# A four-tap convolution moved from VectorE to ScalarE and GpSimd in a state-space and mixture kernel

## The reference, cut to what matters

```
x0  = layernorm(x)                       # then an RMS norm with norm_scale
xs, res = split(rms(x0) @ w_in)          # 512 channels each
xs  = silu(causal_conv(xs, conv_w, 4 taps per channel) + conv_b);  res = silu(res)
delta, B, C = split(xs @ w_xproj);  delta = softplus(delta @ w_dt + b_dt)
state[c, n, t] = exp(delta * A[c, n]) * state[c, n, t-1] + delta * xs * B[n, t]   # 16 states n
y   = sum_n state * C[n];  out = (y + xs * D) * res
x1  = x + layernorm(x0 + out @ w_out)
u   = layernorm(x1)                      # two branches of 8 gated low-rank experts follow,
f   = experts(u, running sum of u)       # each over the running sum along the tokens
result = x1 + layernorm(f @ W_O)
```

## Time and profile before

| what | value |
|---|---|
| median of three runs | 2573.84 us |
| the profiled execution | 2574.76 us, span from first to last instruction 2572.9 us |
| granted TensorE clock, mean | 0.936 |
| busy share of the span | DVE 89%, PE 85%, POOL 68%, ACT 66% |
| first scan to last scan | 95.8 to 2451.8 us, 16 batches |

### The profile page before, as it was taken

The page is one execution under the profiler, slowest core; times in us unless marked ns, Lnnn a source line. Parts: engine busy times, 40 slices in busy tenths (PEclk is TensorE's granted clock), DMA queues, the critical chain, the costliest instruction groups (busy, mean ns, idle before and its releaser), DMA issues.

```text
span 2572.9 us, 35477 instructions
## 1 busy us (share of the span) xinstructions
PE 2179.5 (85%) x9268; PEld 1305.7 (51%) x9268; DVE 2291.9 (89%) x3172; ACT 1704.3 (66%) x3353; POOL 1752.1 (68%) x1227
## 2 busy tenths in 40 slices
PE   5666788888898988888898888989888888888788
PEld 2434455454554645455464545546454555546454
DVE  1599999999999999999899999999999999999941
ACT  3555585958668594876758586685948767595643
POOL 0759586767858676695867768586766958677611
PEclk9776899999999999999899999999999999999999
DMA  5011010101002011110101011020101001011100
GB/s 123 28 46 30 20 58 25 58 26 54 31 20 64 25 56 29 54 30 26 59 25 55 29 54 31 19 64 25 57 28 54 30 26 58 25 50 32 35 1 17
DMA packets 83383, 101.58 MB, mean 39 GB/s; under 512 B 23480, under 2 KB 49872, under 8 KB 83168
## 3 DMA queue, kind: packets, MB, share of 16 engines
q1 hardware_dynamic: 83168, 99.06, 13.1%
HBM read 90.13 MB, written 8.91 MB: 38 GB/s over the span
## 4 chain that ended last, share of the span: by engine, by line
DVE 33%; issue 28%; POOL 15%; PE 15%; ACT 4%; DVEq 1%; POOLq 0%; ACTq 0%
DVE h L1259 15%; POOL bx L714 9%; DVE yT L1275 9%; PE bank L744 8%; PE stateT L913 3%; DVE xs L1163 3%; DVE prod L1234 2%; PE bank L888 2%; POOL x_back L646 1%; POOL scratch L630 1%; POOL scratch L636 1%; DVE xs L1175 1%; ACT decay L1119 1%; DVE rows L1187 1%; ACT cum_sb L1084 1%
## 5 line engine op out<-in xcount | busy, mean ns | idle before, releaser
L714 POOL TENSOR_TENSOR bx<-dx,B_rows 128x1024 f32<-128x1024 f32 x512 | 1206.6, 2363 | 379.3 <-DVE h L1259 374.7
L1259 DVE TENSOR_TENSOR_SCAN h<-decay,bx 128x512 f32<-128x512 f32 x1024 | 1237.7, 1209 | 57.4 <-ACT decay L1119 50.9
L1119 ACT ACTIVATE decay<-delta,decay_rate 128x512 f32<-128x512 f32 x1024 | 706.6, 692 | 487.3 <-DVE h L1259 477.3
L913 PE MATMUL stateT<-ident,h 128*128 128x128 f32 x4096 | 668.8, 295 | 264.9 <-DVE h L1259 179.5
L913 PEld LDWEIGHTS stateT<-ident,h 128*128 128x128 f32 x4096 | 498.8, 149 | 614.5 <-issue 333.2
L1275 DVE SCALAR_TENSOR_TENSOR yT<-stateT,C_tok,yT 128x512 f32<-128x512 f32 x960 | 697.8, 727 | 34.3 <-PE stateT L913 29.7
L744 PE MATMUL bank<-hT,w_in_sb 128*128 128x512 f32 x512 | 247.5, 621 | 34.7 <-DVE xs L1163 33.7
L744 PE MATMUL bank<-k_to_expert,cumT 128*128 128x512 f32 x512 | 266.4, 647 | 4.1 <-DVE prod L1234 4.1
L744 PE MATMUL bank<-q_to_expert,xnT 128*128 128x512 f32 x512 | 248.0, 608 | 1.9 <-ACT C_tok L1007 1.9
L1084 ACT ACTIVATE cum_sb<-bank,gate 128x64 f32<-128x64 f32 x1024 | 222.7, 328 | 35.6 <-PE bank L744 33.3
L888 PE MATMUL bank<-expert_to_out,prodT 128*128 128x256 f32 x1024 | 241.8, 379 | 0.0
(11 more groups left out here) (162 smaller groups left out, 2412.9 us busy)
## 6 DMA issues: line engine op xcount, KB each, us to landing
B_rows<-B_scratch SPq DMA_DIRECT2D x256, 256.0 KB, 3.2
x_front<-in_L_attn_x SPq DMA_DIRECT2D x16, 512.0 KB, 4.6
x_back<-in_L_attn_x SPq DMA_DIRECT2D x16, 512.0 KB, 4.1
out<-x_back SPq DMA_DIRECT2D x16, 512.0 KB, 3.3
w_in_sb<-in_L_attn_w_in SPq DMA_DIRECT2D x1, 1024.0 KB, 5.9
h<-in_L_ffn_V_fwd SPq DMA_DIRECT2D x2, 256.0 KB
h<-in_L_ffn_W_inv_exp SPq DMA_DIRECT2D x2, 256.0 KB
h<-in_L_ffn_W_fwd SPq DMA_DIRECT2D x2, 256.0 KB
```

The costliest lines, as they stand in the source:

```text
L714: pool.tensor_tensor(bx[use % BX_RING][:, :, :], dx[q.parity][:, 2 * half:2 * half + 2, :], row, ALU.mult).then_inc(s_bx.step(f"{n},{half} ...
L913: last = pe.transpose(stateT[j % 2][:, c * P:(c + 1) * P], h[n % 2][:, c, j * P:(j + 1) * P], ident[:, :])
L1119: act.activation(decay[c % 2][:, :], delta[q.parity][:, c, :], ACT.Exp, scale=decay_rate[:, c, n:n + 1]).then_inc(s_exp.step(f"{n},{c}"), 1)
L1259: dve.tensor_tensor_scan(h[n % 2][:, c, :], decay[c % 2][:, :], bx[(2 * n + c // 2) % BX_RING][:, c % 2, :], 0.0, ALU.mult, ALU.add).then_ ...
```

## The change

Four things change.

- **Convolution.** The DVE tasks cvA, cvB and cvC are gone. A new ACT task `tap` makes, for each group of 128 channels, three products from the same PSUM bank (`Copy` with the tap as scale) into a ring of four rows of `scratch`; a new POOL task `cv` adds each of them to `xs`, shifted. Every add waits for its product and for the add before it. From the fifth product on, ACT waits until POOL has added the product four before. The bank is free after the third product. The silu of ACT waits for POOL's last add, and so do the later writers of `scratch`.
- **Front norm.** ACT sums the rows with an accumulator output (`front_sum`) and then squares `sum - 256 x` with another (`front_square`). The unused elementwise results go to `hT`.
- **Output norm.** The copy from PSUM into `o_rows` becomes an `Identity` with an accumulator output, and four squares (`out_square`) follow. POOL's factor instructions take scales for these sums; their number stays.
- **Beats.** The timetable is new for most tasks.

```diff
-    ("F", "cvA", "dve"): (35, 37, 38, 42),
-    ("F", "cvB", "dve"): (37, 37, 39, 42),
-    ("F", "cvC", "dve"): (37, 37, 40, 44),
+    ("F", "sum", "act"): (5,),
+    ("F", "sq", "act"): (10,),
+    ("F", "tap", "act"): (35, 37, 41, 44),
+    ("F", "cv", "pool"): (40, 41, 44, 57),
-    ("F", "xs", "pe"): (34, 35, 37, 40),
+    ("F", "xs", "pe"): (31, 32, 34, 39),
-    ("F", "res", "pe"): (36, 38, 41, 66),
+    ("F", "res", "pe"): (34, 41, 45, 62),
-    ("B", "rb", "pool"): (300,),
+    ("B", "rb", "pool"): (303,),
     ("B", "t", "act"): (301,),
-    ("B", "st1", "dve"): (302,),
+    ("B", "st1", "dve"): (304,),
-    ("L", "out", "pe"): (373, 381, 393, 398, 431, 434, 439, 443),
+    ("L", "out", "pe"): (373, 381, 394, 397, 434, 437, 439, 441),
-    ("L", "st", "dve"): (455,),
-    ("L", "ag", "dve"): (460,),
+    ("L", "sq", "act"): (448,),
...
+            def conv_task(b, c, use):
+                pool.wait_ge(f_act.sem, f_act.done(b, f"cv{c}"))
+                for back in range(1, TAPS):
+                    product = 3 * c + back - 1
+                    pool.wait_ge(f_act.sem, f_act.done(b, f"tp{c}{back}"))
+                    if back > 1:
+                        pool.wait_ge(f_pool.sem, f_pool.done(b, f"cv{c}{back - 1}"))
+                    pool.tensor_tensor(xs[b.parity][:, c, back:], xs[b.parity][:, c, back:], scratch[:, product % 4, 0:T - back],
+                                       ALU.add).then_inc(f_pool.step(f"cv{c}{back}"), 1)
...
+            def front_sum(b, k, use):
+                act.wait_ge(xf_in, b.count(16, 16))
...
+                for j in range(TB):
+                    act.activation(hT[:, j // 2, j % 2 * D:(j % 2 + 1) * D], x_front[:, j, :], ACT.Identity,
+                                   accum_out=sum_f[:, j:j + 1]).then_inc(f_act.step(f"sm{j}"), 1)
+            def front_square(b, k, use):
+                act.wait_ge(f_act.sem, f_act.done(b, "sm3"))
+                for j in range(TB):
+                    act.activation(hT[:, j // 2, j % 2 * D:(j % 2 + 1) * D], x_front[:, j, :], ACT.Square, scale=-1.0 * D, bias=sum_f[:, j:j + 1],
+                                   accum_out=var_f[:, j:j + 1]).then_inc(f_act.step(f"sq{j}"), 1)
...
+            def tap_task(b, c, use):
+                act.wait_ge(f_pe.sem, f_pe.done(b, f"xs{c}"))
+                for back in range(1, TAPS):
+                    product = 3 * c + back - 1
+                    if product >= 4:
+                        before = product - 4
+                        act.wait_ge(f_pool.sem, f_pool.done(b, f"cv{before // 3}{before % 3 + 1}"))
...
+                    act.activation(scratch[:, product % 4, 0:T - back], use.bank[:, 0:T - back], ACT.Copy,
+                                   scale=conv_w_sb[:, c, TAPS - 1 - back:TAPS - back]).then_inc(f_act.step(f"tp{c}{back}"), 1)
...
             def silu_task(b, k, use):
-                act.wait_ge(f_dve.sem, f_dve.done(b, "cvC3"))
+                act.wait_ge(f_pool.sem, f_pool.done(b, "cv33"))
...
-                act.activation(o_rows[:, j, :], use.bank[:, 0:D], ACT.Copy).then_inc(l_act.step(f"out{j}"), 1)
+                act.activation(o_rows[:, j, :], use.bank[:, 0:D], ACT.Identity, accum_out=sum_o[:, j:j + 1]).then_inc(l_act.step(f"out{j}"), 1)
```

More of the change, by code:

```diff
@@ L112 @@
[L112 to L121, removed]
+    ("F", "dt", "act"): (88, 90, 107, 114),
@@ new lines @@
+    ("F", "ex", "act"): (91, 95, 107, 115),
+    ("F", "ln", "act"): (93, 97, 111, 120),
+    ("F", "w", "pool"): (101, 108, 117, 126),
+    ("F", "w2", "pool"): (101, 109, 125, 126),
+    ("F", "d1", "dve"): (96, 105, 120, 123),
+    ("F", "row", "sp"): (95, 128, 132),
+    ("B", "y", "pe"): (263, 264, 264, 264),
+    ("B", "u", "dve"): (264, 264, 264, 269),
+    ("B", "o", "pool"): (273, 275, 277, 278),
+    ("B", "wo", "pe"): (279, 282, 282, 287),
+    ("B", "r", "dve"): (283, 287, 287, 289),
@@ L157 @@
-    ("L", "out", "act"): (382, 401, 440, 445),
-    ("L", "st", "dve"): (455,),
-    ("L", "ag", "dve"): (460,),
-    ("L", "rs", "pool"): (473,),
+    ("B", "logit", "act"): (342,),
+    ("B", "logit_rows", "pe"): (343,),
+    ("B", "lb", "dve"): (342,),
+    ("B", "mx", "dve"): (342,),
+    ("B", "sub", "pool"): (349,),
+    ("B", "ex", "act"): (345,),
+    ("B", "sm", "dve"): (344,),
+    ("B", "sn", "pool"): (354,),
+    ("B", "rc", "dve"): (345,),
+    ("B", "wa", "pool"): (356,),
+    ("B", "gT", "pe"): (367,),
@@ L283, in program @@
         C_tok = [sb(f"C_tok{i}", P, TB, NS) for i in range(2)]
-        st_f, st_b, st_1, st_o = (sb(f"st_{n}", P, TB, 6) for n in "fb1o")
-        mv_f, mv_b, mv_1, mv_o = (sb(f"mv_{n}", P, TB, 2) for n in "fb1o")
+        st_b, st_1 = (sb(f"st_{n}", P, TB, 6) for n in "b1")
+        mv_b, mv_1 = (sb(f"mv_{n}", P, TB, 2) for n in "b1")
+        sum_f, var_f, sum_o, var_o = (sb(n, P, TB) for n in ("sum_f", "var_f", "sum_o", "var_o"))
         ve_f, ms_f, rs_f, r2_f = (sb(n, P, TB) for n in ("ve_f", "ms_f", "rs_f", "r2_f"))
@@ L593, in prologue, with rstd @@
                                allow_small_or_imprecise_dtypes=True))
-            def rstd(steps, batch, mv, ve, rs, nm, names):
-                pool.tensor_scalar(ve[:, :], mv[:, :, 1], EPS, None, ALU.add).then_inc(steps.step(names[0]), 1)
+            def rstd(steps, batch, mean, var, unit, factor, ve, rs, nm, names):
+                pool.tensor_scalar(ve[:, :], var, unit, EPS, ALU.mult, ALU.add).then_inc(steps.step(names[0]), 1)
                 pool.wait_ge(steps.sem, steps.done(batch, names[0]))
@@ L684, in back_rstd @@
                 pool.sem_inc(passed["pool"], 1)
-                rstd(b_pool, b, mv_b, ve_b, rs_b, nm_b, ("ve", "rb", "ng", "nm"))
+                rstd(b_pool, b, mv_b[:, :, 0], mv_b[:, :, 1], 1.0, minus_one, ve_b, rs_b, nm_b, ("ve", "rb", "ng", "nm"))
             def x1_rstd(b, k, use):
@@ L949, in centre, with out_square @@
                     act.activation(dst[:, j, :], src[:, j, :], ACT.Identity, scale=rs[:, j:j + 1], bias=nm[:, j:j + 1]).then_inc(steps.step(f"{name}{j}"), 1)
+            def front_sum(b, k, use):
+                act.wait_ge(xf_in, b.count(16, 16))
+                if b.turn is not None or b.const > 0:
+                    act.wait_ge(B_out, b.count(16, 0))
+                for j in range(TB):
[6 more added lines that the diff above has]
+                                   accum_out=var_f[:, j:j + 1]).then_inc(f_act.step(f"sq{j}"), 1)
+            def out_square(b, k, use):
+                act.wait_ge(l_act.sem, l_act.done(b, "out3"))
+                for j in range(TB):
+                    act.activation(flat(prodT[:, 2 * j:2 * j + 2, :]), o_rows[:, j, :], ACT.Square, scale=-1.0 * D, bias=sum_o[:, j:j + 1],
+                                   accum_out=var_o[:, j:j + 1]).then_inc(l_act.step(f"sq{j}"), 1)
             def h_task(b, k, use):
@@ L1149, in aggregate @@
                     dve.bn_aggr(mv[:, j, :], st[:, j, :]).then_inc(steps.step(f"{name}{j}"), 1)
-            def front_stats(b, k, use):
-                dve.wait_ge(xf_in, b.count(16, 16))
-                stats(f_dve, x_front, st_f, "st")
-            def front_aggregate(b, k, use):
-                aggregate(f_dve, b, st_f, mv_f, "st", "ag")
-            def tap(back, name, before):
-                def task(b, c, use):
-                    x_c = xs[b.parity][:, c, :]
-                    dve.wait_ge(before[0].sem, before[0].done(b, f"{before[1]}{c}"))
-                    dve.scalar_tensor_tensor(out=x_c[:, back:], in0=use.bank[:, 0:T - back], scalar=conv_w_sb[:, c, TAPS - 1 - back:TAPS - back],
-                                             in1=x_c[:, back:], op0=ALU.mult, op1=ALU.add).then_inc(f_dve.step(f"{name}{c}"), 1)
-                return task
             def d1_task(b, c, use):
```

129 lines of the change are left out of this document (61 added, 68 removed), and 6 rows, old and new, of the table TIMETABLE.

## The result

The changed kernel takes 2507.12 us (median of four runs, 2505.18 to 2508.23) against 2573.85 us, a ratio of 0.9737 with a 95% interval of 0.9712 to 0.9762. The forecast was 2479 us: the sign and the range hold, and the gain is 67 us where 96 were forecast. The profiled execution has a span of 2506.4 us against 2572.9; the mean granted TensorE clock is 0.937 against 0.936, and it is 1.00 in beats 24 to 47 of the batches shown, before and after, so the clock doesn't explain the gain.

The account below looks back on a forecast made before the run. DVE was taken to bound the kernel. Fifteen batches each win 11.2 us less 4.5 given back, and the start costs 5: -96 from 2574.76, so 2479 us; range for 8 in 10: 2408 to 2575.

Parts of the forecast that it names:

- What bounds the kernel: Whole kernel: DVE, busy 2291.9 of 2572.9 us, sets the period; in beats 40 to 47 PE is busy throughout.
- Taken from DVE: Per batch: twelve taps 7.9 us, eight bn_stats 2.6, eight bn_aggr 0.7, together 11.2 us less DVE work.
- Given back in beats 24 to 47: Beats 24 to 47: 4.5 us a batch of the DVE saving lost again, range 3.0 to 6.5.
- The account by PE: Beats 24 to 47: PE still needs 30.5 us where DVE needs 25.7, so 3.0 to 4.8 us come back.
- The account by POOL and ACT: From beat 32's scan: beat 46's exponential queues behind cv2, rb and t, so DVE waits 4.9 us.
- Elsewhere: Beats outside 24 to 47: output statistics' 1.7 us on DVE won, squares covered, front sums, Identity and loads cost nothing.
- The start: First batch: its convolution isn't under a scan, POOL's adds end at 52.7, so 5 us are lost once.
- The rule against it: Convolution adds: two-input elementwise work is about twice as slow on GpSimd; 7.9 us of one engine become 23 of two.
- All of it is won: Rival, chance 0.22: PE and POOL catch up in gaps of other slots, nothing given back, 2412 us.
- ACT as the bound in 64 to 95: Rival, chance 0.10: squares, dearer accumulators and dense silu and gelu give back 4.1 us more a batch, 2541 us.
- The tie of ACT to POOL over the ring of four: Rival, chance 0.20: late POOL holds ACT in its taps, so DVE waits for bx and decay; 2605 us, slower.
- The signs named: Beats 32 to 47 some 22 us, DVE idle 4 to 5; mv_b wait gone; new nm_b wait 3 us or more.

Follow-up runs that it names:

- e3: Changed kernel with POOL's twelve convolution adds cut to 8 columns each, ACT's products, waits and order kept: 2498.55 us, ratio 0.9703 to the kernel before.
- e5: Changed kernel with ACT's t (norm of B) at beat 48 instead of 45, behind the exponentials of beats 46 and 48: 2549.74 us.
- e9: Changed kernel with DVE's sixth expert product moved from beat 38 to 40 and PE's xv0 from beat 95 to 97: 2484.50 us.
- e10: As e9, and DVE's third r task also moved from beat 31 to 33: 2485.88 us, ratio 0.9647 to the kernel before.
- e4: Changed kernel with res projections 0 to 2 (beats 34, 41, 45) over one of two channel halves, less work for PE: 2481.39 us.
- e2: Changed kernel with the statistics of both norms back on DVE at old beats 7, 8, 71 and 76, convolution as changed: 2534.84 us.
- e7: Changed kernel with ACT's eight squares a batch cut from 256 to 8 columns, accumulator reads kept: 2505.19 us.
- e8: Changed code with all tasks common to the old timetable back at their old beats, only new tasks at new beats: 2586.11 us.
- e11: Kernel before with only the convolution moved to ACT and POOL, statistics and all other beats as before: 2604.65 us.
- e1: Changed kernel with the convolution back on DVE at its old beats, statistics on ACT and all other beats as changed: 2690.57 us.
- e6: Changed kernel with the first add of each group over 510 columns instead of 511: 2505.52 us (single run).

## Why the prediction was right, and where it was off

**What bounds the kernel.** Held: DVE was the pace, and with it relieved PE became full in beats 24 to 47, named beforehand as the place.

**Taken from DVE.** Forecast 11.2 us a batch, busy time near 2115 us; measured 2126.1, 10.4 a batch. A little less. An instruction of DVE that waits doesn't overlap the one before it in the records, and such gaps (over 0.06 us) rose from 146 to 273; at the 0.08 us of an overlap that makes 0.6 of the 0.8, an estimate.

**Given back in beats 24 to 47.** Forecast 4.5 us by two accounts. The account by PE was the right one: e3 shows that POOL can be 8.5 us shorter there without effect, e5 that the exponential behind t can be freed without effect, e9 and e10 that PE's list fills the stretch to 28.96 us. It was mis-sized: I took PE's list for 30.5 us from its busy time of before, and it is 29.0. Measured is 3.4. e4 bounds the account: with PE relieved further the stretch shrinks by 0.8 us only. The account by POOL and ACT (4.9 us at the exponential of beat 46) was wrong in size, 0.58 measured. Counted from the scan of beat 32, rb ended at 15.0 us where I had 17.8: three tasks of adds took 3.6 us each and not 4.05, and by starting in slot 24 to 31, where DVE already waited for PE, POOL had won another 1.5. And DVE itself came to this scan at 17.4 and not at 15.6, since it had waited for PE on the way. The twelve adds take 13.8 us a batch, below even the lower end of 14.8 that I gave. That t must stand where it stands, as e5 shows, was not in my account.

**Elsewhere.** This is the largest step that failed in the sum: "Elsewhere ... nothing". DVE's idle time a batch (means of ten batches, gaps over 0.06 us) rose from 7.0 to 11.9 us; 3.4 of it lies in beats 24 to 47, where there was 0.1, so 1.6 came up in other slots: +0.8 in 64 to 71 (exponential behind ACT's dense tasks: I had counted the output norm's statistics on DVE as won, and e2 shows that those in this slot were covered by ACT's silu), +1.25 in 96 to 103 (transposes behind xv0, which e9 removes), +0.6 in 56 to 63, and +0.7 in 120 to 127 net of others, against less in 88 to 95 and in slot 0. The squares themselves are not the cause (e7, e2), although I had kept them as a rival.

**Sum.** 150.0 to 144.7 is 5.3 us a batch, not 6.7: 0.8 less taken and 1.6 lost elsewhere, against 1.1 less given back. That the two errors of the forecast partly cancel is luck. From the 1.4 come some 21 of the 28 us missing. The first period and the last ones carried less than a steady batch: the scans' whole stretch shrank by 72 us, from 2356.0 to 2283.9, where 15 x 5.3 would be 80. The start was right: +4.4 for +5.

**What I had not weighed: the beats.** I counted work taken and work given back and took the timetable as the place where this happens. At the old beats the same code gives 2586 us (e8), and the convolution alone 2605 (e11). So the whole gain, and 11 us more, comes only with the new order; 79 us lie between e8 and the changed kernel at nearly equal busy times (PE 9 us apart, the others under 3). The new order gives nothing by itself either, as far as e1 shows it: with the convolution left on DVE it is slower still. Both parts on DVE at the new beats was not run. The forecast came out near because the slot accounts were made for the new order.

**The rule against it.** The Trainium skill (GPSIMD Engine Reference, Engine selection) has two-input elementwise work about twice as slow on GpSimd. The trace agrees in kind, 1271 and 1090 ns against 733, and yet it costs nothing in the steady period here, since POOL waited for DVE at this place (e3: 9 us, all at the start). The rule holds for the price, not for the choice.

**The rivals.** "All of it is won" is out: 2412. "ACT as the bound in 64 to 95" explains 0.8 us a batch. The tie of ACT to POOL over the ring of four didn't come about: ACT's taps waited 2.5 us for POOL in the whole execution.

**The signs named.** Beats 32 to 47 take 20.2 us and not 22, and DVE idles 2.4 in them and not 4 to 5; the largest wait there is `prod` for PE's bank, which I had not named. POOL's wait for mv_b is all but gone, as said: 2 waits in all where there were 16. The new wait of ACT's `rows` for POOL's nm_b, 3 us or more in each batch, didn't come: there are three such waits in all, one of them 10.0 us. DVE's idle time in beats 64 to 95 is 4.5 us a batch, more than in 24 to 47, but it was 4.8 before; only within it did it move.

## What to carry to other kernels

When work leaves the busiest engine of an in-order pipeline, compute for each stretch what the second busiest engine has to do there: the stretch can't become shorter than that. Where that engine is full, moving the instruction that waits only moves the wait (24 to 47 in e9 and e10); where it isn't, a move can win the wait (96 to 103 in e9, where PE was busy for 8.02 of 9.70 us before the move). Work on an engine that was waiting was free here even at 1.5 to 1.7 times the price, but only if each reader and each buffer is planned anew; the same code in the old order gained nothing. Before moving an instruction out of another's way, follow who waits for its result: e5 saved 17 us of one wait and paid 40 for the next.

## What the runs showed of the hardware

An accumulator output on ACT is a second instruction in the trace. Four rows of the front's sums and squares:

```profile
1096.97 0.41 ACT L970 ACTIVATE hT<-x_front 128x256 f32<-128x256 f32 x1
1097.28 0.19 ACT L970 ACTIVATION_READ_ACCUMULATOR hT<-x_front 128x1 f32 x1
1097.37 0.40 ACT L970 ACTIVATE hT<-x_front 128x256 f32<-128x256 f32 x1
...
1104.76 0.24 ACT L976 ACTIVATION_READ_ACCUMULATOR hT<-x_front,sum_f 128x1 f32 x1
```

It is 0.19 to 0.24 us long but the next instruction starts 0.09 after it, so twelve cost 1.1 us a batch (forecast 1.5).

On POOL, the first add of a group of three is 1271 ns long, the second and third, which add into the same tile and wait for the one before, are 1090 and 1087 (medians 1270, 1089 and 1087):

```profile
L633 POOL TENSOR_TENSOR xs<-xs,scratch 128x511 f32<-128x511 f32 x64 | 81.4, 1271 | 10.8 <-ACT scratch L1027 10.8
...
L633 POOL TENSOR_TENSOR xs<-xs,scratch 128x510 f32<-128x510 f32 x64 | 69.7, 1090 | 6.3 <-POOL xs L633 0.4
L633 POOL TENSOR_TENSOR xs<-xs,scratch 128x509 f32<-128x509 f32 x64 | 69.6, 1087 | 6.1
```

e6 rules out the number of columns; what else makes the 0.18 us stays open. Waiting for the instruction before is not enough for it: the softplus adds of L646, also in place, mostly wait so too, and 49 of the 64 take 1.26 to 1.30 us. The other 15 take 1.60 to 1.75. Each of these 15, and none of the 49, runs at the same time as an add of DVE that reads two tiles in SBUF (`delta`, L1205), for 0.47 to 0.61 us. In the kernel before it is the same, 14 long ones of 64. So POOL's add is slower whenever the two meet; by what way, the trace doesn't show.
